# Best-expert stages: the first weight matrix is fetched for each slot tile and becomes the stationary operand

## What is computed

```python
xn = layernorm(x)                       # and once more inside, then * ln_g + ln_b
e = argmax(softmax(xn @ Wr + br))       # one of 8 experts, with its gate g
h = relu(xn2 @ W1[e] + b1[e])           # 128 -> 512
y = g * (h @ W2[e] + b2[e])             # 512 -> 128
x = x + y
```

## Time and profile before

| | |
|---|---|
| median of 3 runs | 3652.19 us (3649.19 to 3654.99) |
| span of the profiled execution | 3648.4 us |
| the profiled execution's own time beside its span | not listed apart; the median is 3.8 us above the span |
| mean granted TensorE clock | 0.915 |
| first expert stage, first L1885 to last `y` | 2547.15 to 2666.24 us |
| second expert stage, the same | 3480.58 to 3599.88 us |
| TensorE, VectorE, ScalarE busy | 77%, 68%, 50% of the span |

### The profile page before, as it was taken

One profiled execution on the slowest core, in us unless ns is written; L12 is line 12 of the kernel. 1 busy time (PEld: TensorE's weight loads), 2 busy tenths in 40 slices (PEclk: granted clock), 3 DMA queues, 4 the chain that ended last, 5 costly groups with the idle time before them and its releaser, 6 DMA issues. The chain is left out here.

```text
span 3648.4 us, 55901 instructions
## 1 busy us (share of the span) xinstructions
PE 2793.5 (77%) x12554; PEld 1301.0 (36%) x12555; DVE 2494.0 (68%) x4119; ACT 1822.6 (50%) x3518; POOL 374.9 (10%) x612
## 2 busy tenths in 40 slices
PE   4695899999996798699999999783834555554374
PEld 3442233333332444255555555372621101101352
DVE  5666777777774667666666666454348999999622
ACT  1113577777775102244444444301216999999121
POOL 1014000000001113000000000103042000000303
PEclk9798899999998698799999999995969999999587
DMA  6003111111112005321122112280112111110012
GB/s 187 1 0 92 41 52 47 50 52 47 50 52 77 26 0 179 123 64 62 62 64 63 64 61 68 62 166 28 43 45 84 32 32 33 33 33 18 16 44 67
DMA packets 162391, 211.87 MB, mean 58 GB/s; under 512 B 35344, under 2 KB 89872, under 8 KB 161872
## 3 DMA queue, kind: packets, MB, share of 16 engines
q1 hardware_dynamic: 158224, 202.65, 18.4%
q0 software_dynamic: 4096, 8.40, 0.8%
HBM read 124.08 MB, written 86.38 MB: 58 GB/s over the span
## 5 line engine op out<-in xcount | busy, mean ns | idle before, releaser
L1068 ACT ACTIVATE prob<-ps 128x512 f32<-128x512 f32 (+3 forms) x1792 | 903.7, 551 | 572.5 <-PE ps L978 304.3
L1118 DVE TENSOR_REDUCE neg_max<-ps 128x1 f32<-128x1024 f32 (+7 forms) x1024 | 991.0, 989 | 177.6 <-PE ps L969 157.3
L1001 PE MATMUL ps<-prob,v 128*32 128x512 f32 (+3 forms) x3584 | 830.9, 567 | 1.3 <-ACT prob L1068 1.3
L1545 DVE TENSOR_REDUCE neg_max<-ps 128x1 f32<-128x1024 f32 x512 | 579.3, 1380 | 6.3 <-PE ps L1528 6.3
L978 PE MATMUL ps<-q_stack,k_stack 128*128 128x512 bf16 (+3 forms) x1792 | 560.8, 362 | 17.8 <-ACT prob L1068 9.9
L1568 ACT ACTIVATE ps<-ps,neg_max 128x1024 f32<-128x1024 f32 x512 | 557.1, 1088 | 10.6 <-DVE neg_max L1545 10.6
L1528 PE MATMUL ps<-k_stack,q_stack 128*128 128x512 bf16 x1024 | 311.1, 386 | 285.0 <-ACT ps L1568 266.6
L969 PE MATMUL ps<-k_stack,q_stack 72*128 72x512 bf16 (+3 forms) x1792 | 455.2, 364 | 57.2 <-DMA v<-v_heads 47.5
L1001 PEld LDWEIGHTS ps<-prob,v 128*32 128x32 f32 (+1 forms) x3584 | 340.6, 171 | 216.8 <-issue 189.6
L1116 DVE TENSOR_TENSOR ps<-ps,mask_qk 128x128 f32<-128x128 f32 x512 | 149.8, 293 | 257.7 <-PE ps L969 257.5
L978 PEld LDWEIGHTS ps<-q_stack,k_stack 128*128 128x128 bf16 x1792 | 154.4, 97 | 453.7 <-ACT prob L1068 353.3
(11 more groups left out here) (246 smaller groups left out, 2733.6 us busy)
## 6 DMA issues: line engine op xcount, KB each, us to landing
q_stack<-q_parts SPq DMA_DIRECT2D x576, 48.0 KB
k_stack<-k_parts SPq DMA_DIRECT2D x576, 48.0 KB
o_wide<-o_out SPq DMA_DIRECT2D x64, 260.0 KB
o_quads<-o_out SPq DMA_DIRECT2D x64, 256.0 KB
v_heads<-v_out SPq DMA_DIRECT2D x4, 4096.0 KB
v<-v_heads SPq DMA_DIRECT2D x64, 256.0 KB
num<-o_wide SPq DMA_DIRECT2D x16, 1024.0 KB
q_parts<-parts SPq DMA_DIRECT2D x24, 384.0 KB
```

The costliest lines, as they stand in the source:

```text
L1001: nc.tensor.matmul(out, vs[j.slot(4)][:, :, kt], prob[:, n % RING, o:GROUP], start=start, stop=stop).then_inc(pv_mm.sem, 1)
L1068: nc.scalar.activation(prob[:, m % RING, o:GROUP], ps[:, S2 + m % 2, o:GROUP], ACT.Exp).then_inc(exped.sem, 1)
L1118: nc.vector.tensor_reduce(neg_max[:, i.slot(2), qt:qt + 1], ps[:, bank:bank + 2, :].rearrange("p b n -> p (b n)")[:, 0:keys], AX.X, ALU.ma ...
L1545: nc.vector.tensor_reduce(neg_max[:, i.slot(2), qt:qt + 1], ps[:, 2 * (qt % 4):2 * (qt % 4) + 2, :], AX.XY, ALU.max, negate=True).then_inc ...
```

## The change

`S.f1_w1` stays in DRAM. SyncE reads the expert number of each slot tile itself and loads that expert's 128x512 matrix (256 KB) into `w1`, which has four buffers, right behind the tile's `xs`. It starts a load two pairs ahead once the first product (`h_mm`) of the pair that used the buffer is done; it was `x_mm`, the transposition, before. TensorE multiplies with a 128x128 piece of `w1` as stationary operand and `xsT` as moving one, so the product is already transposed. The four transpositions for each tile and the buffer `h` are gone. ScalarE adds bias and relu for two of the four pieces ("upper") and VectorE for the other two ("lower"), straight into `hT`; the bias is one number for each partition. On TensorE the step now goes tile by tile: first product of front tile 0, second product of back tile 0, then the same for tile 1. The matrices and the broadcast biases no longer load at the start; a 128x32 table of biases does.

```diff
-    XB, HB, TB, YB = (0, 1), (2, 3), (4, 5), (6, 7)
+    XB, HB, YB = (0, 1), (2, 3, 4, 5), (6, 7)
...
                 def load(j, n):
 
                     for s in (0, 1):
-                        sp.dma_start(xs[:, 2 * n + s, :], S.x_slots[bass.ds((j * 4 + (2 * n + s)) * P, P), :]
+                        t = j * 4 + (2 * n + s)
+                        sp.dma_start(xs[:, 2 * n + s, :], S.x_slots[bass.ds(t * P, P), :]
                                      ).then_inc(loaded[2 * n + s], 16)
+                        e = sp.value_load(S.tile_expert[0:1, bass.ds(t, 1)], min_val=0, max_val=E - 1)
+                        sp.dma_start(w1[:, 2 * n + s, :], S.f1_w1[:, bass.ds(e * F, F)]
+                                     ).then_inc(w1_loaded[2 * n + s], 16)
...
-                        x_mm.wait(sp, j * 4 + (2 * n + 1))
+                        h_mm.wait(sp, (j * 4 + (2 * n + 1)) * 2 + 1)
                         load(j + 1, n)
                         store(j, n)
...
             @block.tensor
             def _(pe):
...
                     if front:
                         j, n = front
-                        e = experts(pe, front)
                         for t, s in tiles(front):
                             pe.wait_ge(loaded[2 * n + s], j * 16 + 16)
                             xT_ready.wait(pe, t - 2)
                             nc.tensor.transpose(ps[:, XB[s], 0:P], xs[:, 2 * n + s, :], S.ident[:]).then_inc(x_mm.sem, 1)
                     if back:
-                        for t, s in tiles(back):
-                            h_ready.wait(pe, t)
-                            hT_ready.wait(pe, t - 2)
-                            for f in range(FC):
-                                op = nc.tensor.transpose(ps[:, TB[s], f * P:(f + 1) * P], h[:, s, f * P:(f + 1) * P],
-                                                         S.ident[:])
-                            op.then_inc(hT_mm.sem, 1)
-                    if front:
-                        for t, s in tiles(front):
+                        e = experts(pe, back)
+                    for s in (0, 1):
+                        if front:
+                            t = j * 4 + (2 * n + s)
                             xT_ready.wait(pe, t)
-                            h_ready.wait(pe, t - 2)
-                            nc.tensor.matmul(ps[:, HB[s], :], xsT[:, s, :], S.f1_w1[:, cols(e[s] * F, F)], start=True,
-                                             stop=True).then_inc(h_mm.sem, 1)
-                    if back:
-                        e = experts(pe, back)
-                        for t, s in tiles(back):
-                            hT_ready.wait(pe, t)
+                            pe.wait_ge(w1_loaded[2 * n + s], j * 16 + 16)
+                            upper_ready.wait(pe, t - 2)
+                            lower_ready.wait(pe, t - 2)
+                            for half in (0, 1):
+                                for f in (0, 1):
+                                    op = nc.tensor.matmul(ps[:, HB[2 * s + half], f * P:(f + 1) * P],
+                                                          w1[:, 2 * n + s, (2 * half + f) * P:(2 * half + f + 1) * P],
+                                                          xsT[:, s, :], start=True, stop=True)
+                                op.then_inc(h_mm.sem, 1)
+                        if back:
+                            t = tiles(back)[s][0]
                             y_ready.wait(pe, t - 2)
...
             @block.scalar
             def _(act):
...
                     if front:
+                        e = experts(act, front)
                         for t, s in tiles(front):
                             x_mm.wait(act, t)
-                            h_mm.wait(act, t - 2)
+                            h_mm.wait(act, t * 2 - 3)
                             nc.scalar.activation(xsT[:, s, :], ps[:, XB[s], 0:P], ACT.Identity, bias=S.f1_lnb[:],
                                                  scale=S.f1_lng[:]).then_inc(xT_ready.sem, 1)
-                    if back:
-                        for t, s in tiles(back):
-                            hT_mm.wait(act, t)
+                        for t, s in tiles(front):
+                            h_mm.wait(act, t * 2)
                             y_mm.wait(act, t - 2)
-                            nc.scalar.activation(hT[:, s, :], ps[:, TB[s], :], ACT.Relu).then_inc(hT_ready.sem, 1)
+                            for f in (0, 1):
+                                op = nc.scalar.activation(hT[:, s, f * P:(f + 1) * P], ps[:, HB[2 * s], f * P:(f + 1) * P],
+                                                          ACT.Relu, bias=S.f1_b1[:, cols(e[s] * FC + f, 1)])
+                            op.then_inc(upper_ready.sem, 1)
...
             @block.vector
             def _(dve):
...
                         for t, s in tiles(front):
-                            h_mm.wait(dve, t)
-                            hT_mm.wait(dve, t - 2)
-                            nc.vector.tensor_tensor(h[:, s, :], ps[:, HB[s], :], S.f1_b1[:, cols(e[s] * F, F)],
-                                                    ALU.add).then_inc(h_ready.sem, 1)
+                            h_mm.wait(dve, t * 2 + 1)
+                            y_mm.wait(dve, t - 2)
+                            for f in (2, 3):
+                                op = nc.vector.tensor_scalar(hT[:, s, f * P:(f + 1) * P],
+                                                             ps[:, HB[2 * s + 1], (f - 2) * P:(f - 1) * P],
+                                                             S.f1_b1[:, cols(e[s] * FC + f, 1)], 0.0, ALU.add, ALU.max)
+                            op.then_inc(lower_ready.sem, 1)
...
-        S.f1_w1, S.f1_b1 = weight("f1_w1", [P, E * 4 * P]), row("f1_b1")
+        S.f1_w1, S.f1_b1 = a["f1_w1"], weight("f1_b1", [P, E * 4])
```

More of the change, by code:

```diff
@@ L1805, in expert_tiles @@
         xsT = sb("xsT", [P, 2, P])
-        h = sb("h", [P, 2, F])
+        w1 = sb("w1", [P, 4, F])
         hT = sb("hT", [P, 2, F])
@@ L1814, in expert_tiles @@
         stored = [sem("stored0"), sem("stored1")]
-        x_mm, xT_ready, h_mm, h_ready, hT_mm, hT_ready, y_mm, y_ready = [steps(n) for n in (
-            "x_mm xT_ready h_mm h_ready hT_mm hT_ready y_mm y_ready").split()]
+        w1_loaded = [sem(f"w1_loaded{n}") for n in range(4)]
+        x_mm, xT_ready, h_mm, upper_ready, lower_ready, y_mm, y_ready = [steps(n) for n in (
+            "x_mm xT_ready h_mm upper_ready lower_ready y_mm y_ready").split()]
         with nc.Block() as block:
@@ L1874, in _ @@
             def _(pe):
-                for s in (x_mm, h_mm, hT_mm, y_mm):
+                for s in (x_mm, h_mm, y_mm):
                     s.open(pe)
@@ L1904, in step @@
                             y_ready.wait(pe, t - 2)
                             for f in range(FC):
+                                if f == 0:
+                                    upper_ready.wait(pe, t)
+                                if f == 2:
+                                    lower_ready.wait(pe, t)
                                 op = nc.tensor.matmul(ps[:, YB[s], 0:P], hT[:, s, f * P:(f + 1) * P],
@@ L1915, in _ @@
                 xT_ready.open(act)
-                hT_ready.open(act)
+                upper_ready.open(act)
                 def step(front, back):
                     if front:
+                        e = experts(act, front)
                         for t, s in tiles(front):
                             x_mm.wait(act, t)
-                            h_mm.wait(act, t - 2)
+                            h_mm.wait(act, t * 2 - 3)
                             nc.scalar.activation(xsT[:, s, :], ps[:, XB[s], 0:P], ACT.Identity, bias=S.f1_lnb[:],
                                                  scale=S.f1_lng[:]).then_inc(xT_ready.sem, 1)
-                    if back:
-                        for t, s in tiles(back):
-                            hT_mm.wait(act, t)
+                        for t, s in tiles(front):
+                            h_mm.wait(act, t * 2)
                             y_mm.wait(act, t - 2)
-                            nc.scalar.activation(hT[:, s, :], ps[:, TB[s], :], ACT.Relu).then_inc(hT_ready.sem, 1)
+                            for f in (0, 1):
+                                op = nc.scalar.activation(hT[:, s, f * P:(f + 1) * P], ps[:, HB[2 * s], f * P:(f + 1) * P],
+                                                          ACT.Relu, bias=S.f1_b1[:, cols(e[s] * FC + f, 1)])
+                            op.then_inc(upper_ready.sem, 1)
                 pairs(act, step)
@@ L1934, in _ @@
             def _(dve):
-                h_ready.open(dve)
+                lower_ready.open(dve)
                 y_ready.open(dve)
@@ L2132, in arrays_of @@
         "f1_w1": g["L1_ffn_W1"].transpose(1, 0, 2).reshape(D, E * 4 * P),
-        "f1_b1": g["L1_ffn_b1"].reshape(E * 4 * P),
+        "f1_b1": T(g["L1_ffn_b1"].reshape(E * 4, P)),
```

## The result

The changed kernel takes 3724.81 us (median of 4 runs, 3719.02 to 3728.77), against 3650.69 us (3647.10 to 3654.99, 4 runs) for the kernel before: 74 us longer, a ratio of 1.0202 (95% interval 1.0188 to 1.0217). The sign of the forecast was right; the time lies 12 us above the range. The profiled execution spans 3727.1 us, 78.7 us more than that of before.

What follows compares the result with a forecast made beforehand. TensorE was taken to bound the expert stages before the change. (6.6 - 5.89) x 19 steps = 13.5, + 1.2 - 0.7 = 14.0 us a stage, 28 for both; 3648.4 + 28 + 3.8 = 3680 us, range 3655 to 3713 us.

Steps and rivals of the forecast that it cites:

- The sign of the forecast: Whole kernel: slower 81%, within 0.2% of no change 9%, faster 10%.
- the range: Whole kernel's forecast time: 3655 to 3713 us.
- What was removed: TensorE in the expert stages: eight transpositions of h a step, 1.09 us, and the front table read with its gap.
- The chain through ScalarE: Expert loop: ScalarE's pieces, reads and x copy wait for the step's last product; a step takes 6.6 us, was 5.89.
- E: Expert loop: the end of a step's last product on TensorE, from which the forecast counts its times.
- 0.1 for the branch: Expert loop: ScalarE's part of the loop's branch, estimated at 0.1 us a step.
- The step that failed: SyncE's loads: second xs lands at E + 7.0, two steps take 12.7 us, 6.4 a step, under 6.6, so no cost.
- TensorE's 1.5 us of reads: Expert loop: after the second xs lands, TensorE needs 1.5 us of table reads before its products.
- the loads bind: Rival, SyncE's loads: second xs lands at E + 8.25, a step takes 7.0 us, 3695 us in all; chance 18%.
- The clock: Rival, TensorE in the expert stages: pauses lower the clock to 0.84, 30 us more, 3710 us; chance 13%.
- one case: Forecast itself, the ScalarE chain setting the step: 3680 us, own range 3668 to 3692 us, chance 50%.
- Start and end: Each expert stage: first product 1.2 us later at the start, 0.7 us less at the end.

Runs made afterwards that it cites:

- edit 12: edit 9 with four hT buffers in place of two, all table reads kept: 3626.21 us, 0.9933 of the kernel before.
- edit 10: edit 9 plus eight unused identity transpositions between a step's two transposed x: 3670.73 us, 1.0059 of the kernel before.
- Edits 11: edit 9 without ScalarE's table reads, one fixed expert's bias columns for every tile: 3637.63 us, 0.9963 of the kernel before.
- edit 1: Changed kernel with both xs loads of a pair issued ahead of its table reads and w1 loads: 3702.95 us, 1.0144 of the kernel before.
- edit 3: Changed kernel with w1 loaded only for the first four slot tiles of each stage: 3690.94 us, 1.0107 of the kernel before.
- edit 9: Changed kernel with eight xs and w1 buffers, four pairs a loop turn, loads four pairs ahead: 3694.6 us, 1.0157 of the kernel before.
- edits 7: edit 1 plus eight unused identity transpositions between a step's two transposed x: 3678.18 us, 1.0071 of the kernel before.
- edit 4: Changed kernel plus eight unused identity transpositions between a step's two transposed x: 3724.91 us, 1.0205 of the kernel before.
- edit 5: Changed kernel with four hT buffers in place of two: 3714.21 us, 1.0174 of the kernel before.

## Why the prediction was right in sign and short in size

**What was removed: right.** The groups of products take 3.84 us a step at full clock (2610.69 to 2614.53), forecast 4.1, so the 16 passes of 128 columns that replace 4 of 512 cost nothing that can be seen. With the waits gone (edit 12) the changed kernel is 24 us under the kernel before, though its loop then also has half as many turns.

**The chain through ScalarE: right in mechanism, 0.5 us too dear.** 2.15 to 2.30 us from E to the product, forecast 2.4 and 0.1 for the branch; 6.11 us a step where nothing else stands in the way (edit 10), forecast 6.6. Edits 11 and 12 take away its two parts, the reads and the wait for `y_mm`, and a step falls to 5.30 and 5.02 us. The chain alone, less what the change saves, costs the 20 us of edit 10, forecast 28.

**The step that failed:** "The second `xs` is issued at E + 2.25 + 0.91 + 0.4 + 0.45 + 0.7 + 0.45 = E + 5.2 ... so it lands at E + 7.0", and from it "it costs nothing by itself, but it is close". It was issued at E + 5.98: the stores begin at E + 2.54, the gap behind them is 0.70 us, and from the first `xs` to the second it is 1.77 us. And it landed 2.90 us after its issue in the step shown, 2.3 to 3.0 us wherever else TensorE waited for a second `xs`, and not 1.83. A 256 KB `w1` stands just ahead of it in the queue. The first `xs` of a pair, with none just ahead, took 1.9 to 2.0 us; with both `xs` first the second is there within 1.9 us (edit 1); and without `w1` the loads took 1.9 to 2.1 us (edit 3), but for one early in each stage with 2.9 and 3.1, which are not explained. So it landed at E + 8.9, where the chain was done with its step at E + 6.0. Every part of that sum came out longer than its row, and the margin was 0.2 us a step (6.4 against 6.6). The two `w1` were also later than forecast: issued at E + 5.4 and E + 7.1, with the median of 2.9 us they land at E + 8.3 and E + 10.0, not at E + 7.4 and E + 9. (The forecast's times for their products, E + 8.6 and E + 10.7, should by its own chain have been E + 9.0 and E + 11.1.) What the prediction had right is what follows the landing, TensorE's 1.5 us of reads with nothing to cover them. The loads are 30 us of the 74 (edit 9). The rival "the loads bind" had the place right and E + 8.25.

**The clock: the rival's size, the wrong bookkeeping.** It was priced at 30 us and measured 24 once the loads were out of the way (edit 9 against 10; 25 for edit 1 against 7), and the forecast's sum had it at nothing. The forecast held one case to be true and the others false, where all three are in the time: taken away in the order loads, clock, chain, the 74 us are 30, 24 and 20. That these make up the whole shows nothing by itself, since the last is what is left, and the split holds for this order alone. With the loads in place, the clock alone gave back nothing (edit 4) and the wait on `hT` 11 us (edit 5). One also feeds the next: the chain's pause alone gave 0.90 in the stretch from 2560 to 2660 us, with the load's pause it was 0.80. The Trainium skill, Perfetto Trace Analysis, Matmul Optimizations, wants matmuls back to back in batches since the engine scales with utilization; edits 7 and 10 agree, with 25 and 24 us less for 1.04 us of added work in each step.

**Start and end: mis-sized.** +1.2 - 0.7 us a stage was forecast beside the steps. The first two steps took 3.0 us longer in the first stage and 0.8 in the second; the end, forecast to be shorter, takes 3.3 and 3.4 us more, for the pause of 2.24 us above and a late load. No gain could be seen from the weights and biases that are no longer loaded at the program's start, as forecast; the first stage begins later, by the 6.7 us above.

**Left open.** Edit 9 has a wide interval, for one of its four runs. Beside it stand edit 3, which puts the loads at 34 us, and edits 1 and 7, which put the clock at 25; with intervals of some 7 us either way, the split is good to no more than that. The kernel before was not given four pairs in a loop turn, so how much of edit 12's lead over it comes from the shorter loop and not from the new products was not measured. Which pause drops the clock, and why not each of the same length does, was not tried, nor was the later start of the first stage.

## What to carry to other kernels

When work leaves the bounding engine, look at what it was covering: here the transposed h had hidden the release of a buffer, and the new last consumer of that buffer put another engine's reads on the path. If several rivals grow out of the same pause, expect them together instead of choosing one, and take them away one on top of the other: removed alone, the clock's part was worth nothing here, and behind the loads it was worth 24 us. A change that loses by its waits may win once its buffers are deeper: the same products with twice the `xs`, `w1` and `hT` buffers, and half the loop turns, went from 1.0202 to 0.9933 of the time before.

## What was not expected of the hardware

- Adding 1.04 us of useless transpositions to each step made the kernel 25 us (edit 1 to 7) and 24 us (edit 9 to 10) faster; the granted clock of the stage went from 0.87-0.91 to 0.97. Where a load set the pace the clock rose too, and the time did not move (edit 4).
- Where TensorE's wait shows the landing of a 64 KB load in the changed kernel, it was 1.8 to 2.0 us after the issue with nothing large just ahead of it, and 2.3 to 3.0 us with a 256 KB load just ahead.
- With the stores of `y` on GpSimd, the first gather started 10.2 us after the last `y` and not 3.1 us; 5.95 us of that is a DRAIN on GpSimd's sequencer, where SyncE's took 7 ns.
